# First stage of an attention kernel: fills moved off GpSimd, query and key handled one by one, the first loads on two queues

## What is computed

```python
def _flash_attn(Q, K, V):
    def body(carry, kv):
        out, m, l = carry
        K_blk, V_blk = kv
        scores = jnp.einsum('bhqd,bhkd->bhqk', Q, K_blk) * SCALE
        M_ij = scores.max(axis=-1, keepdims=True)
        m_new = jnp.maximum(m, M_ij)
        corr = jnp.exp(m - m_new)
        exp_scores = jnp.exp(scores - m_new)
        chunk_sum = exp_scores.sum(axis=-1, keepdims=True)
        l_new = chunk_sum * corr + chunk_sum
        out_new = out * corr + jnp.einsum('bhqk,bhkd->bhqd', exp_scores, V_blk)
        return ((out_new, m_new, l_new), None)
...
Q = split_heads(x @ q_w.T)
K = split_heads(x @ k_w.T)
V = split_heads(x @ v_w.T)
...
x = x + _layernorm(_L0_attn_ref(_layernorm(x, axis=-1), ...), axis=-1)
x = x + _layernorm(_L0_ffn_ref(_layernorm(x, axis=-1), ...), axis=-1)
x = x + _layernorm(_L1_attn_ref(_layernorm(x, axis=-1), ...), axis=-1)
x = x + _layernorm(_L1_ffn_ref(_layernorm(x, axis=-1), ...), axis=-1)
```

## Time and profile before

| | |
|---|---|
| Median of 3 runs | 1690.49 us |
| The runs | 1691.08, 1684.03, 1690.49 us |
| Time of the profiled execution | 1691.9 us |
| Its span in the profile | 1690.1 us |
| TensorE / VectorE / ScalarE / GpSimd busy | 91% / 76% / 69% / 42% |
| First score matmul | 37.42 us after the span's start |

### The profile page before, as it was taken

The page is one execution under the profiler, slowest core; times in us unless marked ns, Lnnn a source line. Parts: engine busy times, 40 slices in busy tenths (PEclk is TensorE's granted clock), DMA queues, the critical chain, the costliest instruction groups (busy, mean ns, idle before and its releaser), DMA issues. The chain is left out here.

```text
span 1690.1 us, 34457 instructions
## 1 busy us (share of the span) xinstructions
PE 1541.2 (91%) x8456; PEld 843.8 (50%) x8456; DVE 1285.4 (76%) x3546; ACT 1166.5 (69%) x2450; POOL 716.7 (42%) x1011
## 2 busy tenths in 40 slices
PE   4999999999999999999979999999999978867995
PEld 2333333333333333333347777777745655544764
DVE  4899999999999999989876777777668863313664
ACT  1488888888888888878867777777635544553663
POOL 2224334344343344422353434333344442554887
PEclk7699999999999999989989999999999988997998
DMA  4232333223223232242000000000020001434552
GB/s 122 57 89 78 90 94 88 82 76 92 85 82 100 71 92 84 76 141 55 22 7 7 1 1 0 0 0 0 20 86 1 1 1 38 159 117 124 143 137 66
DMA packets 83649, 109.24 MB, mean 65 GB/s; under 512 B 15947, under 2 KB 48977, under 8 KB 83552
## 3 DMA queue, kind: packets, MB, share of 16 engines
q1 hardware_dynamic: 77152, 91.28, 19.0%
q0 software_dynamic: 6400, 16.82, 2.8%
HBM read 63.24 MB, written 40.08 MB: 61 GB/s over the span
## 5 line engine op out<-in xcount | busy, mean ns | idle before, releaser
L853 DVE TENSOR_REDUCE bmax<-PS 128x8 f32<-128x512 f32 x1024 | 651.2, 682 | 62.9 <-PE PS L587 60.5
L704 ACT ACTIVATE EX<-PS 128x512 f32<-128x512 f32 x1024 | 564.3, 604 | 105.9 <-PE PS L598 96.5
L587 PE MATMUL PS<-KR,QR 33*128 33x512 f32 x1024 | 410.1, 470 | 36.5 <-DVE bmax L853 23.7
L598 PE MATMUL PS<-QR,KR 64*128 64x512 f32 x1024 | 397.9, 461 | 1.8 <-ACT EX L704 1.5
L587 PEld LDWEIGHTS PS<-KR,QR 33*128 33x128 f32 x1024 | 167.1, 190 | 351.1 <-DVE bmax L853 296.5
L608 PE MATMUL PS<-EX,VS 128*9 128x512 f32 x2048 | 271.6, 602 | 0.0
L598 PEld LDWEIGHTS PS<-QR,KR 64*128 64x128 f32 x1024 | 162.4, 186 | 11.9 <-ACT EX L704 10.2
L1029 PE MATMUL PS<-pA,wb 128*128 128x512 f32 x640 | 151.7, 393 | 0.0
L789 POOL TENSOR_TENSOR m_diff<-m_prev,m_all 128x16 f32<-128x16 f32 x64 | 14.2, 222 | 314.3 <-DVE m_all L865 314.3
L1204 ACT ACTIVATE gelud<-PS,scales 128x512 f32<-128x512 f32 x128 | 88.2, 689 | 64.0 <-PE PS L1029 63.9
L1029 PEld LDWEIGHTS PS<-pA,wb 128*128 128x128 f32 x640 | 118.4, 188 | 23.8
(11 more groups left out here) (231 smaller groups left out, 2806.5 us busy)
## 6 DMA issues: line engine op xcount, KB each, us to landing
QR<-q_scr SPq DMA_DIRECT2D x256, 64.0 KB, 2.5
KR<-k_scr SPq DMA_DIRECT2D x256, 64.0 KB, 2.4
big<-row_scr SPq DMA_DIRECT2D x72, 192.5 KB, 2.3
k_scr<-partsB SPq DMA_DIRECT2D x42, 256.0 KB, 2.9
q_scr<-partsB SPq DMA_DIRECT2D x28, 256.0 KB, 2.9
X<-in_L_attn_x SPq DMA_DIRECT2D x16, 256.0 KB, 2.9
X<-x SPq DMA_DIRECT2D x16, 256.0 KB, 2.5
xB<-in_L_attn_x SPq DMA_DIRECT2D x14, 256.0 KB, 3.3
```

The costliest lines, as they stand in the source:

```text
L587: pe.matmul(PS[:, bank_of(i, n), :], QR[rows, i, h // 2, t * P:(t + 1) * P], KR[rows, i, h // 2, :], start=True, stop=True).then_inc(tile_ ...
L598: pe.matmul(PS[:, RING3 + bank_of(j, n), :], KR[rows, j, h // 2, kt * P:(kt + 1) * P], QR[rows, j, h // 2, :], start=True, stop=True).then ...
L704: act.activation(EX[:, n % (2 * HG), :], PS[:, RING3 + bank_of(j, n), :], ACT.Exp, scale=SCALE).then_inc(ex_set, 1)
L853: dve.tensor_reduce(bmax[:, i % 2, n, :], PS[:, bank_of(i, n), :].rearrange("p (b k) -> p b k", k=BLK), AX_X, ALU.max).then_inc(tile_max, 1)
```

## The change

- `parts` now holds one chunk, `partsB` is created earlier and takes chunk 1's pieces (`pieces = (parts, partsB)`). Whoever writes `partsB` or loads chunk 1 in the second block first waits for chunk 1's stores; the wait at the first block's end is gone.
- GpSimd fills `QR` as its first work; ScalarE fills `KR`, as the first work too, from `neg_half` (which holds -0.5, times 2).
- Query and key are copied, subtracted and stored one after the other, each on its own semaphore count. TensorE turns chunk 1 and only then multiplies value of chunk 0.
- The eight loads of group 0 are split in two halves of four (`load_half`). SP issues one half right behind chunk 0's stores and ahead of chunk 1's, ScalarE the other, between chunk 0's and chunk 1's copies; both wait for chunk 0's stores and for both fills.

```diff
+        partsB = sb("partsB", [P, 2, NPART, S], F32R, att)
...
+        def load_half(eng, b, i, a):
+            heads = slice(i * HG + a, (i + 1) * HG, 2)
+            for r in range(2):
+                rows = slice(HALF * a + r * NPART * HD, HALF * a + (r + 1) * NPART * HD)
+                eng.dma_start(QR[rows, i].bitcast(F32), q_scr[ds(b, 1), heads]
+                              .rearrange("b h j d t -> (j d) (b h) t")).then_inc(load_in[i], 16)
+                eng.dma_start(KR[rows, i].bitcast(F32), k_scr[ds(b, 1), heads, r:r + NPART]
+                              .rearrange("b h j d t -> (j d) (b h) t")).then_inc(load_in[i], 16)
...
-        parts = sb("parts", [P, 2, NPART, 2 * S], F32R, p1)
+        parts = sb("parts", [P, 2, NPART, S], F32R, p1)
+        pieces = (parts, partsB)
...
+                def store_parts(c):
+                    for w in range(2):
+                        for j in range(NPART + w):
+                            if j % NPART == 0:
+                                sp.wait_ge(part1_set, 2 * c + w + 1)
+                            else:
+                                sp.wait_ge(part2_set, 2 * c + w + 1)
+                            sp.dma_start((q_scr, k_scr)[w][ds(c, 1), :, j].rearrange("b h d t -> (b h) d t"),
+                                         pieces[c][:, w, j % NPART, :].bitcast(F32)).then_inc(parts_out[c], 16)
...
-                for c in range(AHEAD):
-                    store_parts(c, c)
+                store_parts(0)
                 sp.wait_ge(parts_out[0], PARTS_DMA)
                 sp.wait_ge(kones, 2)
-                load_group(sp, 0, 0)
-                sp.wait_ge(parts_out[1], PARTS_DMA)
+                load_half(sp, 0, 0, 0)
+                store_parts(1)
...
+                    for w, weights in enumerate((wq, wk)):
+                        if c:
+                            pe.wait_ge(part2_set, 2 * c + w - 1)
+                        pe.matmul(PS[:, 2 + w, :], weights[:], xT1[:, s, :], start=True, stop=True).then_inc(qk_done, 1)
...
+                def cast(c, w):
+                    act.wait_ge(qk_done, 2 * c + w + 1)
+                    act.copy(pieces[c][:, w, 0, :], PS[:, 2 + w, :]).then_inc(part1_set, 1)
...
+                act.wait_ge(ones_set, 1)
+                act.activation(KR[:].rearrange("p i a t -> p (i a t)"),
+                               neg_half[:, 0:1].broadcast_to([P, NG * 2 * S]), ACT.Copy, scale=2.0).then_inc(kones, 1)
...
             def _(pool):
+                pool.memset(QR[:].bitcast(F32), 0.0).then_inc(kones, 1)
                 pool.wait_ge(ones_set, 3)
                 for c in range(AHEAD):
                     rstd(ln1)(pool, c)
-
-                pool.memset(QR[:].bitcast(F32), 0.0).then_inc(kones, 1)
-                pool.memset(KR[:].bitcast(F32), -1.0).then_inc(kones, 1)
...
+                def split(c, w):
+                    dve.wait_ge(part1_set, 2 * c + w + 1)
+                    dve.tensor_tensor(pieces[c][:, w, 1, :], PS[:, 2 + w, :],
+                                      pieces[c][:, w, 0, :], ALU.subtract).then_inc(part2_set, 1)
...
+                    elif i == 0 and isinstance(b, int) and b == 1:
+                        sp.wait_ge(parts_out[1], PARTS_DMA)
...
+                    elif w == 0:
+                        act.wait_ge(parts_out[1], PARTS_DMA)
```

More of the change, by code:

```diff
@@ L212, in block_kernel @@
         vs_preset = sem("vs_preset")
+        def load_half(eng, b, i, a):
[6 more added lines that the diff above has]
+                              .rearrange("b h j d t -> (j d) (b h) t")).then_inc(load_in[i], 16)
         def load_group(sp, b, i):
             for a in range(2):
[L216 to L222, removed]
+                load_half(sp, b, i, a)
         p1 = ExitStack()
@@ L285, in project, with values @@
                     pe.wait_ge(xT1_set, c + 1)
[L286 to L291, removed]
+                    for w, weights in enumerate((wq, wk)):
+                        if c:
+                            pe.wait_ge(part2_set, 2 * c + w - 1)
+                        pe.matmul(PS[:, 2 + w, :], weights[:], xT1[:, s, :], start=True, stop=True).then_inc(qk_done, 1)
+                def values(c, s):
                     for t in range(NT):
@@ L299, in _ @@
                 turn(1, 1)
+                values(0, 0)
                 project(1, 1)
+                values(1, 1)
             @block.scalar
@@ L308, in copy_xT, with copy_v @@
                     act.copy(xT1[:, s, :], PS[:, s, :]).then_inc(xT1_set, 1)
[L310 to L314, removed]
+                def cast(c, w):
+                    act.wait_ge(qk_done, 2 * c + w + 1)
+                    act.copy(pieces[c][:, w, 0, :], PS[:, 2 + w, :]).then_inc(part1_set, 1)
+                def copy_v(c, s):
                     act.wait_ge(v_done, c + 1)
                     act.copy(chunk_of(V, c), PS[:, 4 + s, :]).then_inc(v_set, 1)
+                act.wait_ge(ones_set, 1)
+                act.activation(KR[:].rearrange("p i a t -> p (i a t)"),
+                               neg_half[:, 0:1].broadcast_to([P, NG * 2 * S]), ACT.Copy, scale=2.0).then_inc(kones, 1)
                 copy_xT(0, 0)
                 cast(0, 0)
+                cast(0, 1)
                 copy_xT(1, 1)
+                copy_v(0, 0)
+                act.wait_ge(parts_out[0], PARTS_DMA)
+                act.wait_ge(kones, 2)
+                load_half(act, 0, 0, 1)
+                cast(1, 0)
                 cast(1, 1)
+                copy_v(1, 1)
             @block.gpsimd
             def _(pool):
+                pool.memset(QR[:].bitcast(F32), 0.0).then_inc(kones, 1)
                 pool.wait_ge(ones_set, 3)
@@ L343, in norm @@
                     layernorm(dve, c, ln1, lambda t: tile_of(X, c, t), lambda t: xn1[:, s, t * P:(t + 1) * P])
-                def split(c, s):
-                    dve.wait_ge(part1_set, c + 1)
-                    if late(c, 2):
-                        dve.wait_ge(parts_out[s], (c - s) * (PARTS_DMA // 2))
-                    dve.tensor_tensor(parts[:, s, 1, :], PS[:, 2:4, :].rearrange("p a b -> p (a b)"),
-                                      parts[:, s, 0, :], ALU.subtract).then_inc(part2_set, 1)
+                def split(c, w):
+                    dve.wait_ge(part1_set, 2 * c + w + 1)
+                    dve.tensor_tensor(pieces[c][:, w, 1, :], PS[:, 2 + w, :],
+                                      pieces[c][:, w, 0, :], ALU.subtract).then_inc(part2_set, 1)
                 norm(0, 0)
@@ L354, in _ @@
                 split(0, 0)
+                split(0, 1)
                 dve.memset(VS[:], 0.0).then_inc(vs_preset, 1)
@@ L359, in _ @@
                 dve.memset(VS[BLK:P, :, NT - 1, :, HD], 1.0).then_inc(vs_preset, 1)
+                split(1, 0)
                 split(1, 1)
@@ L378, in block_kernel @@
         xTB = sb("xTB", [P, S], F32, p2)
-        partsB = sb("partsB", [P, 2, NPART, S], F32R, p2)
         ln1b = ln_bufs("ln1b", p2, LN_SPLIT)
```

8 lines of the change are left out of this document (removed).

## The result

The changed kernel takes **1678.02 us** (median of 7, 1675.51 to 1682.1) against 1689.23 us for the kernel before on the same chip (median of 7): a ratio of 0.9936, 95% interval 0.9923 to 0.9948, 11.2 us less. Measured a second time, on the chip of some of the experiments, it gave 0.9934 (0.9910 to 0.9958).

What follows compares the result with a forecast made beforehand. TensorE, 91% busy, was taken as the limit, with a chain of waits delaying its first scores. Starting them 10.6 us earlier took 1691.9 to 1681.3; allowing 1.4 for the profiled run against the median gave 1680.0, range 1673 to 1687.

Steps and rivals of the forecast that it cites:

- The stall and its size: Chunk 1's normalisation on VectorE waits for GpSimd's fills; without them it takes 1.12 instead of 7.52 us, ending 6.4 earlier.
- The upper bound of 0.3 us: At the kernel's start, GpSimd's QR fill could delay VectorE's small first fills by at most 0.3 us; 0 was taken.
- Rival E: First block: the stall has another cause and stays, so only the new order gains; about 1686 us, chance 0.05.
- The chain to the first score: First block: the waits before TensorE's first score matmul shorten, so it starts at 26.8 instead of 37.4 us.
- the first term: First block: chunk 0's last store lands 3.6 us after issue, at 20.45 us, between 19.95 and 21.35.
- A: Group 0's loads: the two queues cost each other or ScalarE issues slowly, 1.9 us more; 1682.3 us, chance 0.14.
- C: First block: GpSimd's preparation after its fill is partly uncovered, first row scale up to 3.6 us late; 1683, chance 0.05.
- D: Attention stage from its third group: the clock rises much later, 1.2 us per four tiles; slower than before, chance 0.04.
- xB: the mis-sized term: Second block: VectorE's wait for the xB load after six reductions was taken as 0, upper bound 1 us.
- the 10.6: The forecast gain in us: first score at 26.8 instead of 37.4, assumed to last through the rest of the kernel.
- TensorE's pace in the first block: Chunk 1's products run at the pace of before, with key ready at 21.9 us, 1.0 ahead of ScalarE.
- B: Start of the attention stage: TensorE's clock rises one to three steps earlier in the work; 1676.3 to 1678.7, chance 0.12.

Runs made afterwards that it cites:

- e1: The kernel before with only the two fills moved, QR's first on GpSimd and KR's first on ScalarE; ratio to before 0.9976.
- e2: The changed kernel with both fills put back on GpSimd behind its power operations; ratio to before 0.9962.
- e3: The changed kernel with KR's fill alone put back on GpSimd behind its power operations; ratio to before 0.9942.
- e5: The changed kernel with both fills first on GpSimd and none on ScalarE; ratio to before 0.9934.
- e9: The changed kernel with query and key copied and subtracted together in 1024 columns again, stores behind the subtraction; ratio to before 0.9961.
- e10: The changed kernel with ScalarE's chunk 1 copies ahead of its wait and loads, and SP's five chunk 1 stores ahead of its loads; ratio to before 0.9915.
- e7: The changed kernel with ScalarE's chunk 1 query and key copies ahead of its wait and its four loads; ratio to before 0.9924.
- e4: The changed kernel with all eight loads of group 0 on SP, ahead of chunk 1's stores; ratio to before 0.9941.
- e6: The changed kernel with chunk 2's X and xB loads issued in the first block, behind chunk 1's x; ratio to before 0.9925.
- changed_again: The changed kernel, unedited, measured again on the chip of some experiments; median 1679.45 us, ratio to before 0.9934.
- e11: The changed kernel with early chunk 1 copies, early X and xB loads, and chunk 1's two query stores ahead of SP's loads; 1675.61 us, ratio 0.9914.

## Why the prediction was right, step by step

**The stall and its size: right.** The trace of the changed kernel and e1, e2, e3 and e5 agree on one mechanism: VectorE's instruction stands until GpSimd's fill is over. The Trainium skill (SBUF — State Buffer, "Who interferes with whom") says so of copies, casts and TENSOR_SCALARs in their two-port forms; e5 shows it for the cast, and VectorE's two fills at 0.81 and 1.08 us, as long beside GpSimd's as before (0.06 and 0.91 us), show the other side, an instruction that does not stop. The upper bound of 0.3 us for them was not needed. But the 6.4 us of the stall were worth 5.2 to 5.3 at the first score (e1, e2), as TensorE's and ScalarE's work for query and key ran beside part of it, and in e1 1.8 of them came through TensorE's clock. Rival E's 1686, which took the whole 6.4 us off, was priced too high by that: with the stall back, 5.7 us are left, not 4.2 (e2).

**The chain to the first score: 26.8 forecast, 26.50 measured.** ScalarE's fill took 3.62 (3.6), the half-width subtraction 0.69 (0.65), ScalarE's loads 0.47 each from start to start as SP's do. Chunk 0's stores landed at 20.07 (20.45), the first term off by more than 0.2: 3.2 us after the last issue, where I took 3.6. From the end of SP's last issue (25.82) to the first score it took 0.68, where the sum had 0.7. Rivals A, C, D and E did not come.

**What is left when the parts are undone one at a time:** fills 5.2 (e2), one by one 5.0 (e9), the loads ahead of the stores 1.5 (e10 against e7, with the copies early), the second queue 1.0 (e4), and one of the fills on ScalarE, not on GpSimd, 1.7 to 1.8 (e5). They overlap and are not a sum.

**xB: the mis-sized term.** I took 0 with an upper bound of 1 us; it was 1.09, and e6 gives it back when the load is moved. xB took 5.1 us from issue to its reader, more than the 3.6 to 4.5 of the earlier trace rows. It stood behind the last stores and X; before, with the last store issued 5.6 us ahead of it, the same load landed 3.4 us after its issue. This term cancels the 0.3 us won on the way to the first score and more: at the third copy of the accumulator the changed kernel is 10.2 us ahead. That the 10.6 came out so near is in part luck: the loss at xB was met by 0.3 us from the stores' landing and 0.4 from the clock, and none of the three was in the sum.

**TensorE's pace in the first block: wrong, with no effect on the time.** I let TensorE run chunk 1's products at the pace of before and had key ready at 21.9, 1.0 us ahead of ScalarE. Its value products took 1.05 us for eight at 18.24, against 1.91: the level of 2.4 GHz. The clock had risen in this block before too, at 16.7 us, and fell at 20.1, behind TensorE's idle 2.8 us; now it rises at 15.7, TensorE works without a pause from 11.1 to 19.3 us, and all of chunk 1's products run at 2.4. Key was ready near 18.4, and ScalarE's wait, not TensorE, held chunk 1. e7 shows it: 0.7 us.

**The clock at the start of the attention stage: a part of what B named, small.** The rise came 1.5 us behind the first product with V, before 3.0. Over the fourteen executions in the table column D goes from 60.6 to 62.4 us as column C goes from -0.7 to +3.5, 0.4 us for each us of delay. changed and changed_again lie at the same place, so it may be systematic for this kernel; with one or two executions each that is not shown. It gave the changed kernel 0.4 us. The Trainium skill (TensorE: Matmul & The Clock Gate, "What's actually happening") says the moment varies from run to run; two executions of one kernel, +1.5 and +1.4, don't show that, and those of different kernels don't test it.

**Where the profiled executions differ by more than the medians.** The two spans differ by 13.9 us, the medians by 11.2: the traced execution of before lies 2.7 us above its median, that of changed at it. What the spans have beyond the start is in one place: up to the attention loop's exit the changed kernel's lead stays at 10.2 to 10.4 us, and then it grows to 14.2. Busy time and clock in stretches of 2 us, before, around the exit:

```profile
744.00:746.00 2.00, 0.87 (x5) 0.36 (x3) 0.82 (x3) 0.20 (x1) 0.00 (x0) 1.00 0.11 33
746.00:748.00 2.00, 1.96 (x11) 0.41 (x11) 1.70 (x4) 1.08 (x2) 0.32 (x2) 0.80 0.95 289
...
752.00:754.00 2.00, 2.00 (x11) 0.89 (x9) 1.62 (x8) 0.90 (x2) 1.03 (x2) 0.50 0.00 0
```

and the same place of the changed kernel:

```profile
734.00:736.00 2.00, 1.44 (x12) 0.49 (x12) 1.18 (x3) 0.84 (x2) 0.00 (x0) 1.00 0.67 188
736.00:738.00 2.00, 1.53 (x12) 0.68 (x8) 2.00 (x5) 1.84 (x5) 0.83 (x4) 1.00 0.91 296
...
740.00:742.00 2.00, 1.58 (x11) 0.59 (x13) 2.00 (x9) 1.76 (x6) 0.99 (x2) 1.00 0.19 31
```

Before, TensorE worked 0.87 of 2 us and then fell to 1.2 GHz for about ten us; in the changed kernel it worked 1.44 of 2 us there and stayed at 2.4. The four groups around the exit took 53.5 us in before and 49.6 in changed. In e1 they took 52.3, with a fall of 6.8 us, and in e6 51.8, with one of 3.4 us; in the other kernels, without a fall, 49.8 to 50.8, and 50.0 in changed_again, whose median was 10.7 us under before's. If before always lost those 3.8 us there and the changed kernel never, the medians would differ by about 14 us; they differ by 11.2 (8.8 to 13.0) and 10.7 (7 to 15). So a constant gain of the change is unlikely, by the first pair alone. Whether it is pure chance stays open: before and e1, which share the order of stores and loads, show the longer falls, e6 with the changed order shows a short one, only one execution of each was traced, and no run isolates it. The start gives 10.2 us; the 0.5 to 1.0 us up to the medians is within their intervals.

## What to carry to other kernels

A fill that nobody waits for is still not free where it runs: beside it on GpSimd, a scaling or a cast on VectorE stands still until the fill is over, so such fills belong where VectorE idles, or on ScalarE. A stall can cost twice: while TensorE idled for it, the granted clock fell, and the products behind it took twice as long (e1). A wait should sit behind the work that others need: ScalarE's copies ahead of its wait (e7), a load issued while the queue is empty (e6) and stores filling a queue's idle time, but not the whole of them ahead of the loads (e10, e11). These last three rest on places in the traces; the times do not tell them apart.

## What had not been expected of the hardware

- Issuing a load of 64 KB cost 0.34 to 0.45 us on either queue in the changed kernel. Right behind five stores of 256 KB SP's first two cost 0.71 and 1.04 us before and 0.78 and 0.86 in e10, where ScalarE's at the same moment cost 0.82 and 0.89.
- For 30.4 us TensorE was busy 28.36 us, mostly with score tiles of 33 rows, and stayed at 1.2 GHz; in the changed kernel's first block the clock rose at 15.7 us, with TensorE at work since 11.1.
- A cast of 128 columns took 2.67 us instead of 0.23 beside a fill on GpSimd (e5).
